# A graph layer's gather stage: the node inputs added by an identity product, the destinations unpacked first, the gathers written out

## The chip, the cores and the metric

One core of one Trainium2 chip runs the whole program. Its engines are PE (TensorE, matrix products), DVE (VectorE), ACT (ScalarE), POOL (GpSimd, which here issues all indirect DMAs) and SP (SyncE, which issues the plain DMAs). Each has an instruction queue of its own, and they wait for one another by semaphores. The metric is the time of one execution on the device in microseconds (us); less is better.

## What is computed

One layer over a graph of 6250 nodes with 256 features and 100,000 directed edges, in float32:

```
xn  = layernorm(x)
deg = count of edges with src != dst per dst node, plus 1
gnn[s] = sum over edges and self loops (s, d) of rsqrt(deg[s]) * rsqrt(deg[d]) * (xn @ W)[d]
mix = linear attention of xn (8 heads, elu + 1), times wo, plus bo
x1  = x + gnn + mix
out = x1 + mixture of 8 experts of layernorm(x1), the best two per node
```

## The kernel before

The nodes are 49 tiles of 128 (`NT`), `P` is 128 and `D` 256. In order of time the program sorts the edges into 25 groups by source (`NGR`; one group is two tiles of source nodes) while it normalizes x and makes keys, values and queries; then comes the **gather stage**, 461 to 1639 us, with which this change deals; then the second norm, the router and the experts.

Before the gather stage, `xn @ W` scaled by `rsqrt(deg)` is written to a DRAM tensor `table`, one row per node (SP, line 357). The sorted edges lie in DRAM as packed words of source and destination, in rows of four, 128 edges to a **chunk**, every chunk within one group. Rows that no edge has filled hold zeros; the places left over are padding edges with source and destination 6400, beyond the last table row, 6271.

Unpacking (lines 763 to 779, DVE; lines 1308 to 1314, PE). Line 365 brings the words to the chip, one chunk per row of 128. DVE splits them into sources and destinations, marks edges from a node to itself, clamps the destination to the last row (line 768) and forms `lo_f`, the source's place in its group. PE transposes `dst_f` and `lo_f` by 16 products with the identity, so that a chunk is a column of 128 partitions, and DVE copies the results to `dst_T` and `lo_neg`.

Then 880 chunks follow (`CHUNKS`), in batches of four (`UNROLL`), four batches to a step (`BATCHES`), 55 steps (`STEPS`). For each chunk:
- ACT copies four indices per batch from `dst_T` to a small buffer `idx_s` (`indices`, line 1131), once the gathers that used that buffer have landed.
- POOL issues one indirect DMA per chunk that gathers 128 rows of `table` into one of sixteen places in `G` (`gather_batch`, line 491). It waits for the indices, and, every second chunk, for PE to be done with the place (`seg`). This is a hardware loop over steps.
- ACT makes a matrix `OH` of ones and zeros that says which source a row belongs to (`onehots`, lines 1133 to 1139).
- PE multiplies (`sum_chunks`, line 1350): two f32 products per chunk, each 128x128 by 128x256 and in two passes, into one of four PSUM banks B[0] to B[3].
- DVE adds the bank, 128x512, to the accumulator `ACC` at the chunk's group (`add_sums`, line 794; the adds run through the helper at line 542). The group's number is unpacked on DVE's queue from a word that it loads for every batch (line 783).

The attention of one tile is woven into each of the first 49 steps: ACT `query_terms`, PE `query_products` (line 1324), DVE `divide` (after the step's first batch), PE `transpose_mix` (line 1331), ACT `transposed_mix`, PE `mix_out` (lines 1337 and 1339: bias, then two products with `wo`, into bank B[7]). In the next step DVE's `add_attention` (line 752) adds B[7] times `sdeg`, the root of the degree, to the tile's accumulator, after the second batch; after the third, `add_inputs` (line 760) adds x times `sdeg`. The order of DVE's step is written out by hand:

```
add_sums(i * BATCHES);      divide(i)
add_sums(i * BATCHES + 1);  add_attention(i - 1)
add_sums(i * BATCHES + 2);  add_inputs(i)
add_sums(i * BATCHES + 3)
```

In the loops, waits on a value that depends on the step go through the helper `when` (lines 102 to 111). In the later expert stage POOL's queue is written out without a loop: per tile a scatter (line 517), a gather of gates (line 510) and one of inputs (line 506).

Of the kernel before, what the change touches and what calls it, by code (L numbers as in the profile page):

```python
# [14 lines left out]
F32, BF16, I32, I16 = mybir.dt.float32, mybir.dt.bfloat16, mybir.dt.int32, mybir.dt.int16  # L15
# [4 lines left out]
P = 128  # L20
N_NODES = 6250
D = 256
# [79 lines left out]
def when(eng, tick, sem, value):  # L102

    if not isinstance(value, int):
        eng.wait_ge(sem, value)
        eng.sem_inc(tick, 1)
    elif value > 0:  # L110
        eng.wait_ge(sem, value)
# [13 lines left out]
def gps_layer(nc, x, src, dst, src_rest, dst_rest, gnn_w, wq, bq, wkv, bkv, wo, bo,  # L125
              wr, br, ln_gT, ln_bT, w1, b1, w2, b2, out):
    ctx = ExitStack()
    with ctx:
# [3 lines left out]
        def sem(name):  # L132
            return ctx.enter_context(nc.semaphore(name))

        def dram(name, shape, dt):
            return nc.dram_tensor(name, shape, dt, kind="Internal").ap()


        table = dram("table", [NT * P, D], F32)
        edge_rows = dram("edge_rows", [CPAD * RPC, ROW], I32)  # L140
# [16 lines left out]
        def piece(area, at, n, dt=F32):  # L157

            words = n if dt in (F32, I32) else (n + 1) // 2
            ap = area[:, at:at + words]  # L160
            return ap if dt == F32 else ap.bitcast(dt)
# [7 lines left out]
        def small(k, n=NT, dt=F32):  # L169
# [61 lines left out]

        raw, src_u, dst_u, same = (piece(BIG, 1024 * k, CPAD, I32) for k in range(4))
        raw3 = grid(BIG, 0, CG, P, I32)
        lo_f, dst_f, same_f = piece(BIG, 1024, CPAD), piece(BIG, 2048, CPAD), piece(BIG, 3072, CPAD)
        G = [grid(BIG, UNROLL * D * s, UNROLL, D) for s in range(BATCHES)]
# [3 lines left out]
        iota2 = piece(W2A, S2 + 3232, GN)  # L239
        idx_s = [piece(W2A, S2 + 3784 + UNROLL * s, UNROLL, I32) for s in range(BATCHES)]  # L240

# [63 lines left out]
            sem("q_terms"), sem("q_ps"), sem("q_mixed"), sem("q_mixedT_ps"), sem("q_mixedT"), sem("q_out"), sem("q_added"))  # L305
        raw_in, unpacked, unp_T, unp_out = sem("raw_in"), sem("unpacked"), sem("unp_T"), sem("unp_out")
        idx_ready, gath, onehot_ready, seg, added = (
            sem("idx_ready"), [[sem(f"gath{s}_{k}") for k in range(UNROLL // 2)] for s in range(BATCHES)], sem("onehot_ready"), sem("seg"), sem("added"))
        w1_in, w2_in, lnb_in, b2_in = [sem(f"w1_in{s}") for s in range(4)], sem("w2_in"), sem("lnb_in"), sem("b2_in")
# [18 lines left out]
        def _(sp):  # L328
# [4 lines left out]
            with nc.allow_non_contiguous_dma(reason="one edge per partition"):  # L333
# [15 lines left out]
                         ).then_inc(cleared_edges, 16)  # L349
            sp.dma_start(gates.rearrange("(c p) o -> c (p o)", p=P)[PICKS:PICKS + 1, :], zeros[0:1, 0:P]).then_inc(gates_out, 16)  # L350
            sp.wait_ge(cgroup_row, 1)
            sp.dma_start(chunk_groups.rearrange("(j p) -> j p", p=P // UNROLL), chunk_wI).then_inc(cgroup_out, 16)

            for k in range(TPARTS):
                sp.wait_ge(table_ready, k + 1)
                ts_ = slice(k * TPART, (k + 1) * TPART)
                sp.dma_start(table.rearrange("(t p) d -> p t d", p=P)[:, ts_, :], acc[:, ts_, :]).then_inc(table_out, 16)

# [64 lines left out]
        def _(pool):  # L423
# [59 lines left out]

            pool.wait_ge(table_out, 16 * TPARTS)

            def gather_batch(n, h):
                when(pool, tk_g, idx_ready, n + 1)
                for u in range(UNROLL):
                    if u % 2 == 0:
                        when(pool, tk_g, seg, (n - BATCHES) * UNROLL + u + 2)  # L490
                    pool.indirect_dma_start(G[h][:, u, :], None, table,  # L491
                                            bass.IndirectOffsetOnAxis(ap=idx_s[h][:, u:u + 1], axis=0)).then_inc(gath[h][u // 2], 16)

            for h in range(BATCHES):
                gather_batch(h, h)
            with pool.Fori(1, STEPS) as i:
                for h in range(BATCHES):
                    gather_batch(i * BATCHES + h, h)

# [38 lines left out]
        def _(dve):  # L538
            ch = Chain(dve, dve_steps)

            def tt(o, a, b, op):
                return dve.tensor_tensor(o, a, b, op)  # L542

            def ts(o, a, s1, op0, s2=None, op1=ALU.bypass):
                return dve.tensor_scalar(o, a, s1, s2, op0, op1)  # L545
# [208 lines left out]

            def add_inputs(t):

                dve.drain()
                a = acc[:, bass.ds(t, 1), :].rearrange("p o d -> p (o d)")
                xt = xr[:, bass.ds(t, 1), :].rearrange("p o d -> p (o d)")
                dve.scalar_tensor_tensor(out=a, in0=xt, scalar=sdeg[:, bass.ds(t, 1)], in1=a, op0=ALU.mult, op1=ALU.add)  # L760


            dve.wait_ge(raw_in, 16)
            ch.add(ts(src_u, raw, CODE, ALU.logical_shift_right))
            ch.add(ts(dst_u, raw, (1 << CODE) - 1, ALU.bitwise_and))
            ch.sync()
            ch.link(tt(same_f, src_u, dst_u, ALU.is_equal))
            ch.add(ts(dst_f, dst_u, float(NT * P - 1), ALU.min))
            ch.link(ts(raw, src_u, GN - 1, ALU.bitwise_and))

            ch.link(dve.scalar_tensor_tensor(out=lo_f, in0=same_f, scalar=float(2 * GN), in1=raw, op0=ALU.mult, op1=ALU.add))
            dve.sem_inc(unpacked, 1)
            for k in range(4):
                dve.wait_ge(unp_T, k + 1)
                n = min(512, CHUNKS - 512 * (k % 2))
                to = (dst_T, lo_neg)[k // 2][:, 512 * (k % 2):512 * (k % 2) + n]
                ch.add(dve.tensor_copy(to, B[k][:, 0:n]) if k < 2 else ts(to, B[k][:, 0:n], -1.0, ALU.mult))
            ch.sync()
            dve.sem_inc(unp_out, 1)
# [16 lines left out]
            def add_step(i):  # L796

                add_sums(i * BATCHES)
                if not isinstance(i, int) or i < NT:
                    divide(i)  # L800
                add_sums(i * BATCHES + 1)
                if not isinstance(i, int) or i > 0:
                    add_attention(i - 1)
                add_sums(i * BATCHES + 2)
                if not isinstance(i, int) or i < NT:
                    add_inputs(i)
                add_sums(i * BATCHES + 3)
# [4 lines left out]

            dve.wait_ge(table_out, 16 * TPARTS)
            add_step(0)
# [221 lines left out]
        def _(act):  # L1036
# [89 lines left out]

            def indices(n, h):

                for half in gath[h]:
                    when(act, tk_a, half, (n - h) * (32 // BATCHES))  # L1130
                act.copy(idx_s[h], dst_T[:, bass.ds(n * UNROLL, UNROLL)]).then_inc(idx_ready, 1)

            def onehots(n, h):
# [7 lines left out]
            def index_step(i):  # L1141
                for h in range(BATCHES):
                    if h == 3 and (not isinstance(i, int) or i > 0):
                        transposed_mix(i - 1)
                    indices(i * BATCHES + h + 1, (h + 1) % BATCHES)
                    if h < 3 and (not isinstance(i, int) or i < NT):
                        query_terms(i, h)
                    onehots(i * BATCHES + h, h)

            act.wait_ge(unp_out, 1)  # L1150
            indices(0, 0)
            index_step(0)
            with act.Fori(1, NT) as i:
                index_step(i)
            index_step(NT)
            with act.Fori(NT + 1, STEPS - 1) as i:
                for h in range(BATCHES):
                    indices(i * BATCHES + h + 1, (h + 1) % BATCHES)
                    onehots(i * BATCHES + h, h)
            for h in range(BATCHES):  # L1160
                if h < BATCHES - 1:
                    indices((STEPS - 1) * BATCHES + h + 1, h + 1)
                onehots((STEPS - 1) * BATCHES + h, h)


# [63 lines left out]
        def _(pe):  # L1229
# [77 lines left out]

            pe.wait_ge(unpacked, 1)
            for k in range(4):
                f = (dst_f, lo_f)[k // 2]  # L1310
                for j in range(4):
                    c = (k % 2) * 4 + j
                    last = nc.tensor.transpose(B[k][:, j * P:(j + 1) * P], f[:, c * P:(c + 1) * P], ident)
                last.then_inc(unp_T, 1)
# [19 lines left out]
            def mix_out(t):  # L1334
                when(pe, tk_t, q_mixedT, t + 1)
                when(pe, tk_t, q_added, t)
                mm(B[7][:, 0:D], ones_b, bias3[:, 2 * D:3 * D], start=True, stop=False)
                for g in range(KD):
                    last = mm(B[7][:, 0:D], mixedT[:, g, :], wo_s[:, g, :], start=False, stop=g == KD - 1)  # L1339
                last.then_inc(q_out, 1)  # L1340
# [161 lines left out]
```

## Time and profile before

| what | us |
|---|---|
| runs, median of 3 (lowest, highest) | 2579.94 (2579.68, 2581.04) |
| the profiled execution | 2579.8 |
| its span, first to last instruction | 2577.9 |
| PE busy in the span | 2203.5 |
| POOL busy | 1495.1 |
| DVE busy | 1313.0 |
| ACT busy | 1193.6 |

All times in rows count from the span's start. PE's busy time is that of pipelined products and their ends are modelled. A timeline row gives start, duration, engine, line, operation, the tiles written and read, a count, and in brackets the engine's idle time before it with what ended that; the name in the brackets is inferred, and it may be an engine that had been done long before.

### The profile page before, as it was taken

The page shows a single profiled execution, that of the slowest core. Times are in us where ns is not written, and L with a number is a line of the kernel's source. Part 1 is how long each engine was busy: PE and PEld are TensorE (multiplying, and loading weights), DVE is VectorE, ACT ScalarE, POOL GpSimd, SP SyncE. Part 2 cuts the span into 40 slices and gives each one's busy share as a digit, 9 for nine tenths or more (in the row PEclk, how much of TensorE's full clock was granted, in tenths as well). Part 3 has the DMA queues.
Part 4 walks back from the last instruction along what each step waited for, and adds up shares of the span by engine and source line. Part 5 has one row for each costly group of instructions (what it writes and reads, how often), then busy time and mean ns, then how long its engine had stood idle before and what let it go on. Part 6 is the DMA issues. An engine that isn't in the chain of part 4 may idle for free.

```text
span 2577.9 us, 54413 instructions
## 1 busy us (share of the span) xinstructions
PE 2203.5 (85%) x12043; PEld 1767.6 (69%) x12044; DVE 1313.0 (51%) x2361; ACT 1193.6 (46%) x3065; POOL 1495.1 (58%) x1493
## 2 busy tenths in 40 slices
PE   0999995788888888888888886658999999999995
PEld 0677774666666666666666664554999999999995
DVE  8799997555555555555555564543122222222221
ACT  2444442566666666666666664462233333322221
POOL 6766565677777777777777776101544444444442
PEclk9999997899999999999999999756999999999998
DMA  4000003233333333333333338455666666666664
GB/s 137 1 1 1 1 1 113 86 104 105 99 99 98 99 98 99 98 98 100 98 99 98 99 118 82 81 182 182 213 183 183 181 180 178 178 180 182 183 183 134
DMA packets 140076, 298.89 MB, mean 116 GB/s; under 512 B 31634, under 2 KB 80868, under 8 KB 139783
## 3 DMA queue, kind: packets, MB, share of 16 engines
q0 software_dynamic: 72672, 143.45, 22.5%
q1 hardware_dynamic: 67367, 155.03, 18.5%
q8 instruction: 12, 0.20, 0.0%
q14 instruction: 25, 0.20, 0.0%
HBM read 264.21 MB, written 40.58 MB: 118 GB/s over the span
## 4 chain that ended last, share of the span: by engine, by line
PE 58%; DVE 14%; DVEq 11%; issue 8%; DMA 4%; POOL 4%; ACT 0%; POOLq 0%; SPq 0%; ACTq 0%
PE B L1350 21%; PE B L1443 15%; PE B L1452 14%; DVE ACC L542 5%; DVEq L660 5%; DVE BIG L655 4%; DMA BIG<-table,W2A 3%; DVEq L783 2%; PE B L1339 2%; PE B L1324 2%; PE B L1412 1%; PE B L1390 1%; DVEq L791 1%; DVE W1A L542 1%; POOL W2A L467 1%
## 5 line engine op out<-in xcount | busy, mean ns | idle before, releaser
L491 POOL DMA_INDIRECT BIG<-table,W2A x880 | 834.3, 948 | 349.8 <-issue 223.5
L542 DVE TENSOR_TENSOR ACC<-ACC,B 128x512 f32 x880 | 605.4, 688 | 448.1 <-PE B L1350 320.7
L1350 PE MATMUL B<-BIG 128*128 128x256 f32 x1760 | 438.7, 393 | 106.8 <-DVE ACC L542 64.8
L1350 PE MATMUL B<-BIG,W2A 128*128 128x256 f32 x1760 | 437.6, 390 | 86.7 <-DVE ACC L542 55.7
L1040 ACT ACTIVATE BIG<-B,SMALL 128x128 f32<-128x128 f32 (+1 forms) x889 | 251.2, 388 | 524.0 <-PE B L1443 524.0
L1350 PEld LDWEIGHTS B<-BIG 128*128 128x128 f32 x1760 | 305.9, 190 | 238.9 <-issue 206.8
L1350 PEld LDWEIGHTS B<-BIG,W2A 128*128 128x128 f32 x1760 | 301.6, 189 | 199.7 <-issue 167.1
L1443 PEld LDWEIGHTS B<-BIG,W1A 128*128 128x128 f32 x3360 | 393.5, 193 | 7.9 <-DVE BIG L545 2.6
L1443 PE MATMUL B<-BIG,W1A 128*128 128x128 f32 x3360 | 394.3, 276 | 2.0 <-DVE BIG L545 2.0
L1452 PE MATMUL B<-W2A,BIG 128*128 x1680 | 380.2, 379 | 0.9 <-DVE BIG L542 0.7
L517 POOL DMA_INDIRECT sums<-BIG,SMALL x105 | 170.6, 1625 | 334.5 <-DMA sums<-BIG,SMALL 289.1
L1452 PEld LDWEIGHTS B<-W2A,BIG 128*128 128x128 f32 x1680 | 311.0, 190 | 39.4 <-issue 1.5
L1040 ACT ACTIVATE BIG<-W2A 128x256 f32<-128x256 f32 x440 | 187.6, 497 | 233.2 <-PE B L1350 233.2
L477 POOL DMA_INDIRECT edge_rows<-BIG x216 | 219.8, 1018 | 126.7 <-DVE BIG L665 64.6
L1040 ACT ACTIVATE W2A<-W2A 128x256 f32<-128x256 f32 x440 | 187.4, 496 | 203.8 <-PE B L1350 203.8
L545 DVE TENSOR_SCALAR BIG<-B,SMALL 128x128 f32<-128x128 f32 x210 | 76.5, 406 | 291.0 <-PE B L1431 291.0
L542 DVE TENSOR_TENSOR BIG<-B,W1A 128x256 f32<-128x256 f32 x105 | 44.6, 424 | 272.8 <-PE B L1452 272.8
L1040 ACT ACTIVATE BIG<-B 128x256 f32<-128x256 f32 (+1 forms) x172 | 65.7, 412 | 201.7 <-PE B L1256 166.3
L506 POOL DMA_INDIRECT BIG<-token_x,SMALL x53 | 51.1, 964 | 173.9 <-DVEq L982 158.0
L1040 ACT ACTIVATE BIG<-BIG,CONST 128x1024 f32<-128x1024 f32 x110 | 126.5, 1150 | 8.1
L1040 ACT ACTIVATE W2A<-W2A,CONST 128x1024 f32<-128x1024 f32 x110 | 126.4, 1149 | 8.1
L510 POOL DMA_INDIRECT BIG<-gates,SMALL x105 | 102.9, 980 | 32.0 <-issue 32.0
(214 smaller groups left out, 2198.0 us busy)
## 6 DMA issues: line engine op xcount, KB each, us to landing
W1A<-in_w SPq DMA_DIRECT2D x105, 1024.0 KB, 5.1
BIG<-table,W2A POOLq DMA_INDIRECT x880
W2A<-in_w SPq DMA_DIRECT2D x1, 8192.0 KB, 30.1
sums<-ACC SPq DMA_DIRECT2D x1, 6400.0 KB, 22.7
table<-ACC SPq DMA_DIRECT2D x7, 896.0 KB, 7.1
out_dram<-sums SPq DMA_DIRECT2D x1, 6250.0 KB, 21.9
W2A<-in_x SPq DMA_DIRECT2D x1, 6144.0 KB
token_x<-BIG SPq DMA_DIRECT2D x24, 256.0 KB, 2.1
```

The source lines that it names most:

```text
L477: pool.indirect_dma_start(edge_rows, bass.IndirectOffsetOnAxis(ap=row_at[s][:, j:j + 1], axis=0), stage_raw[s][:, ROW * j:ROW * (j + 1)], ...
L491: pool.indirect_dma_start(G[h][:, u, :], None, table, bass.IndirectOffsetOnAxis(ap=idx_s[h][:, u:u + 1], axis=0)).then_inc(gath[h][u // 2] ...
L510: pool.indirect_dma_start(slot_gate[:, t:t + 1], None, gates, bass.IndirectOffsetOnAxis(ap=slot_pick[:, t:t + 1], axis=0)).then_inc(gate_i ...
L517: pool.indirect_dma_start(sums, bass.IndirectOffsetOnAxis(ap=slot_row[:, t:t + 1], axis=0), y_out[t % 2], None, compute_op=ALU.add).then_i ...
L542: return dve.tensor_tensor(o, a, b, op)
L545: return dve.tensor_scalar(o, a, s1, s2, op0, op1)
L655: dve.max(eight, work)
L660: dve.drain()
L1040: return nc.scalar.activation(o, i, fn, **kw)
L1350: last = mm(B[u][:, k * D:(k + 1) * D], OH[h % 2][:, u, k * P:(k + 1) * P], G[h][:, u, :], start=True, stop=True)
L1443: last = mm(B[2 * s + c // 4][:, c % 4 * P:(c % 4 + 1) * P], w1_buf[s4][:, k, c * P:(c + 1) * P], x_inT[s][:, k, :], start=k == 0, stop=k ...
L1452: last = mm(B[7][:, 0:D], hidT[s][:, k, :], W2A[:, bass.ds(e * (KH * D) + k * D, D)], start=k == 0, stop=k == KH - 1)
```

## The change

Three things are changed, all in the gather stage.

1. `add_inputs` is removed from DVE's step. In `mix_out` PE multiplies the identity by the tile's x (`xr`) into the same bank B[7], between the bias and the products with `wo`, so that `add_attention` adds both.
2. DVE unpacks the destinations first: mask, copy to f32, and a semaphore for PE, which transposes them while DVE takes out the sources and compares. The two copies to `dst_T` come next and a new semaphore `dst_known`; only then are the sources masked and `lo_f` formed, transposed and copied. The clamp is gone: `table` has two more tiles of rows, which SP fills with zeros early on, and the padding edges read row 6400 there. Some temporary buffers have moved.
3. POOL's gathers are written out, 880 of them, with the index read from `dst_T` itself. `indices` and its buffers on ACT are removed, and with them the wait for the earlier gathers of the same buffer.

```diff
-        table = dram("table", [NT * P, D], F32)
+        table = dram("table", [(NT + 2) * P, D], F32)
...
+            sp.dma_start(table[NT * P:(NT + 2) * P, :].rearrange("(a p) d -> p a d", p=P), zeros.unsqueeze(1).to_broadcast([P, 2, D])
+                         ).then_inc(table_out, 16)
             sp.wait_ge(cgroup_row, 1)
...
-            pool.wait_ge(table_out, 16 * TPARTS)
-
-            def gather_batch(n, h):
-                when(pool, tk_g, idx_ready, n + 1)
-                for u in range(UNROLL):
-                    if u % 2 == 0:
-                        when(pool, tk_g, seg, (n - BATCHES) * UNROLL + u + 2)
-                    pool.indirect_dma_start(G[h][:, u, :], None, table,
-                                            bass.IndirectOffsetOnAxis(ap=idx_s[h][:, u:u + 1], axis=0)).then_inc(gath[h][u // 2], 16)
-
-            for h in range(BATCHES):
-                gather_batch(h, h)
-            with pool.Fori(1, STEPS) as i:
-                for h in range(BATCHES):
-                    gather_batch(i * BATCHES + h, h)
+            pool.wait_ge(table_out, 16 * (TPARTS + 1))
+
+            pool.wait_ge(dst_known, 1)
+            for c in range(CHUNKS):
+                h, u = c // UNROLL % BATCHES, c % UNROLL
+                if u % 2 == 0 and c >= BATCHES * UNROLL:
+                    pool.wait_ge(seg, c - BATCHES * UNROLL + 2)
+                pool.indirect_dma_start(G[h][:, u, :], None, table,
+                                        bass.IndirectOffsetOnAxis(ap=dst_T[:, c:c + 1], axis=0)).then_inc(gath[h][u // 2], 16)
...
-            ch.add(ts(src_u, raw, CODE, ALU.logical_shift_right))
-            ch.add(ts(dst_u, raw, (1 << CODE) - 1, ALU.bitwise_and))
-            ch.sync()
-            ch.link(tt(same_f, src_u, dst_u, ALU.is_equal))
-            ch.add(ts(dst_f, dst_u, float(NT * P - 1), ALU.min))
-            ch.link(ts(raw, src_u, GN - 1, ALU.bitwise_and))
-
-            ch.link(dve.scalar_tensor_tensor(out=lo_f, in0=same_f, scalar=float(2 * GN), in1=raw, op0=ALU.mult, op1=ALU.add))
+            ch.link(ts(dst_u, raw, (1 << CODE) - 1, ALU.bitwise_and))
+            ch.link(dve.tensor_copy(dst_f, dst_u))
             dve.sem_inc(unpacked, 1)
+            ch.link(ts(src_u, raw, CODE, ALU.logical_shift_right))
+            ch.link(tt(lo_f, src_u, dst_u, ALU.is_equal))
...
+            unpacked_half(0)
+            unpacked_half(1)
+            ch.sync()
+            dve.sem_inc(dst_known, 1)
+            ch.link(ts(src_u, src_u, GN - 1, ALU.bitwise_and))
+            ch.link(dve.scalar_tensor_tensor(out=lo_f, in0=lo_f, scalar=float(2 * GN), in1=src_u, op0=ALU.mult, op1=ALU.add))
+            dve.sem_inc(unpacked, 1)
+            unpacked_half(2)
+            unpacked_half(3)
...
-                if not isinstance(i, int) or i < NT:
-                    add_inputs(i)
...
-            pe.wait_ge(unpacked, 1)
             for k in range(4):
+                pe.wait_ge(unpacked, k // 2 + 1)
...
                 mm(B[7][:, 0:D], ones_b, bias3[:, 2 * D:3 * D], start=True, stop=False)
+                mm(B[7][:, 0:D], ident, xr[:, bass.ds(t, 1), :].rearrange("p o d -> p (o d)"), start=False, stop=False)
                 for g in range(KD):
```

`unpacked_half(k)` is the body of the old loop over the four copies. DVE's wait for `table_out` is raised by the same one write, and `index_step` on ACT loses its calls of `indices`.

## Rows read from the trace of the kernel before

**Rows 1.** Stretches (us from the start): each engine's busy time, clock, DMA share, GB/s.
```profile
core 0: us, PE busy (x) PEld busy (x) DVE busy (x) ACT busy (x) POOL busy (x), PEclk, DMA share, GB/s
461.00:657.00 196.00, 164.88 (x716) 121.30 (x717) 113.29 (x188) 125.23 (x267) 148.01 (x156) 0.97 0.35 104
657.00:1518.00 861.00, 736.81 (x3198) 523.34 (x3197) 513.65 (x850) 527.79 (x1131) 612.70 (x647) 1.00 0.33 98
1554.00:1639.00 85.00, 50.85 (x208) 37.45 (x208) 36.45 (x53) 36.35 (x71) 46.44 (x49) 1.00 0.87 78
```

**Rows 2.** Timeline of DVE over one step: start, duration, idle time before it.
```profile
1020.51 0.69 DVE L542 TENSOR_TENSOR ACC<-ACC,B 128x512 f32 x1 [0.90 <-PE B L1350]
...
1030.42 0.48 DVE L752 SCALAR_TENSOR_TENSOR ACC<-B,SMALL,ACC 128x256 f32 x1 [0.42 <-issue]
1031.67 0.69 DVE L542 TENSOR_TENSOR ACC<-ACC,B 128x512 f32 x1 [0.77 <-PE B L1350]
...
1034.83 0.69 DVE L542 TENSOR_TENSOR ACC<-ACC,B 128x512 f32 x1 [0.36 <-PE B L1350]
1035.83 0.48 DVE L760 SCALAR_TENSOR_TENSOR ACC<-W2A,SMALL,ACC  x1 [0.31 <-issue]
1037.08 0.69 DVE L542 TENSOR_TENSOR ACC<-ACC,B 128x512 f32 x1 [0.77 <-PE B L1350]
...
1041.82 0.69 DVE L542 TENSOR_TENSOR ACC<-ACC,B 128x512 f32 x1 [0.90 <-PE B L1350]
```

**Rows 3.** Timeline of PE in that step, and an unhindered batch near the attention's end.
```profile
1016.89 3.97 PE L1350 MATMUL B<-BIG 128*128 128x256 f32 x16 [1.44 <-DVE ACC L542]
...
1025.85 1.13 PE L1339 MATMUL B<-W1A 128*128 128x256 f32 x4
...
1519.63 3.62 PE L1350 MATMUL B<-BIG,W2A 128*128 128x256 f32 x16
```

**Rows 4.** Timeline of POOL: a gather early in the stage, then three in one step.
```profile
655.93 0.95 POOL L491 DMA_INDIRECT BIG<-table,W2A  x1 [0.30 <-issue]
...
684.47 0.94 POOL L491 DMA_INDIRECT BIG<-table,W2A  x1 [1.00 <-PE B L1350]
...
695.91 0.95 POOL L491 DMA_INDIRECT BIG<-table,W2A  x1 [0.30 <-PE B L1350]
...
700.07 0.95 POOL L491 DMA_INDIRECT BIG<-table,W2A  x1 [0.70 <-issue]
```

**Rows 5.** Timeline of all engines at the stage's start.
```profile
450.95 1.29 DVE L545 TENSOR_SCALAR BIG<-BIG 128x1024 int32<-128x1024 int32 x2 [11.59 <-DMA BIG<-edge_rows]
...
456.20 3.68 PE L1313 MATMUL B<-CONST,BIG 128*128 128x128 f32 x16 [35.87 <-DVEq L772]
457.36 0.69 DVE L777 CAST W2A<-B 128x512 int32<-128x512 f32 x1 [1.26 <-PE B L1313]
...
460.61 0.29 ACT L1131 COPY W2A<-W2A 128x4 int32<-128x4 int32 x2 [37.61 <-DVEq L779]
...
461.60 0.99 POOL L491 DMA_INDIRECT BIG<-table,W2A  x1 [23.18 <-ACT W2A L1131]
...
465.73 4.84 PE L1350 MATMUL B<-BIG 128*128 128x256 f32 x10 [5.85 <-DMA BIG<-table,W2A]
```

**Rows 6.** Timeline at the stage's end: a gather on POOL, DVE's last add.
```profile
1551.51 0.95 POOL L491 DMA_INDIRECT BIG<-table,W2A  x1 [0.30 <-issue]
...
1638.29 0.69 DVE L542 TENSOR_TENSOR ACC<-ACC,B 128x512 f32 x1 [0.36 <-issue]
```

**Rows 7.** Timeline before the stage: POOL's scatters, and DVE's multiplication of the table.
```profile
351.87 0.96 POOL L477 DMA_INDIRECT edge_rows<-BIG  x1 [0.30 <-issue]
...
424.02 13.56 DVE L542 TENSOR_TENSOR ACC<-ACC,SMALL 128x1792 f32<-128x1792 f32 x7
...
434.86 1.63 POOL L477 DMA_INDIRECT edge_rows<-BIG  x1 [0.30 <-issue]
```

**Rows 8.** Waits of POOL in the expert stage: us in total, times, longest.
```profile
POOL BIG L510 <- issue: 32.0, 105, 0.3
...
POOL sums L517 <- issue: 12.4, 3, 4.4
```

**Rows 9.** The chain that ended last, share of the span by line.
```profile
PE B L1350 21%; PE B L1443 15%; PE B L1452 14%; DVE ACC L542 5%; DVEq L660 5%; DVE BIG L655 4%; DMA BIG<-table,W2A 3%; DVEq L783 2%; PE B L1339 2%; PE B L1324 2%; PE B L1412 1%; PE B L1390 1%; DVEq L791 1%; DVE W1A L542 1%; POOL W2A L467 1%
```

More of the change, by code:

```diff
@@ L229, in gps_layer @@
         q_den = piece(W1A, S1 + 2480, KD * NH)
-        raw, src_u, dst_u, same = (piece(BIG, 1024 * k, CPAD, I32) for k in range(4))
+        raw, dst_f, dst_u = piece(BIG, 0, CPAD, I32), piece(BIG, 1024, CPAD), piece(BIG, 2048, CPAD, I32)
         raw3 = grid(BIG, 0, CG, P, I32)
-        lo_f, dst_f, same_f = piece(BIG, 1024, CPAD), piece(BIG, 2048, CPAD), piece(BIG, 3072, CPAD)
+        src_u, lo_f = piece(BIG, 4098, CPAD, I32), piece(W2A, S2 + 2 * CHUNKS, CPAD)
         G = [grid(BIG, UNROLL * D * s, UNROLL, D) for s in range(BATCHES)]
@@ L239, in gps_layer @@
         iota2 = piece(W2A, S2 + 3232, GN)
-        idx_s = [piece(W2A, S2 + 3784 + UNROLL * s, UNROLL, I32) for s in range(BATCHES)]
         NE = NT * E
@@ L305, in gps_layer @@
             sem("q_terms"), sem("q_ps"), sem("q_mixed"), sem("q_mixedT_ps"), sem("q_mixedT"), sem("q_out"), sem("q_added"))
-        raw_in, unpacked, unp_T, unp_out = sem("raw_in"), sem("unpacked"), sem("unp_T"), sem("unp_out")
-        idx_ready, gath, onehot_ready, seg, added = (
-            sem("idx_ready"), [[sem(f"gath{s}_{k}") for k in range(UNROLL // 2)] for s in range(BATCHES)], sem("onehot_ready"), sem("seg"), sem("added"))
+        raw_in, unpacked, unp_T, unp_out, dst_known = sem("raw_in"), sem("unpacked"), sem("unp_T"), sem("unp_out"), sem("dst_known")
+        gath, onehot_ready, seg, added = (
+            [[sem(f"gath{s}_{k}") for k in range(UNROLL // 2)] for s in range(BATCHES)], sem("onehot_ready"), sem("seg"), sem("added"))
         w1_in, w2_in, lnb_in, b2_in = [sem(f"w1_in{s}") for s in range(4)], sem("w2_in"), sem("lnb_in"), sem("b2_in")
@@ L356, in _ @@
                 ts_ = slice(k * TPART, (k + 1) * TPART)
-                sp.dma_start(table.rearrange("(t p) d -> p t d", p=P)[:, ts_, :], acc[:, ts_, :]).then_inc(table_out, 16)
+                sp.dma_start(table[0:NT * P, :].rearrange("(t p) d -> p t d", p=P)[:, ts_, :], acc[:, ts_, :]).then_inc(table_out, 16)
             sp.dma_start(wo_s, wo.rearrange("(k p) n -> p k n", p=P)).then_inc(wo_in, 16)
@@ L753, in add_attention, with unpacked_half @@
                                          op0=ALU.mult, op1=ALU.add).then_inc(q_added, 1)
[L755 to L760, printed above, removed]
-            dve.wait_ge(raw_in, 16)
-            ch.add(ts(src_u, raw, CODE, ALU.logical_shift_right))
-            ch.add(ts(dst_u, raw, (1 << CODE) - 1, ALU.bitwise_and))
-            ch.sync()
-            ch.link(tt(same_f, src_u, dst_u, ALU.is_equal))
-            ch.add(ts(dst_f, dst_u, float(NT * P - 1), ALU.min))
-            ch.link(ts(raw, src_u, GN - 1, ALU.bitwise_and))
-            ch.link(dve.scalar_tensor_tensor(out=lo_f, in0=same_f, scalar=float(2 * GN), in1=raw, op0=ALU.mult, op1=ALU.add))
+            dve.wait_ge(raw_in, 16)
+            ch.link(ts(dst_u, raw, (1 << CODE) - 1, ALU.bitwise_and))
+            ch.link(dve.tensor_copy(dst_f, dst_u))
             dve.sem_inc(unpacked, 1)
-            for k in range(4):
+            ch.link(ts(src_u, raw, CODE, ALU.logical_shift_right))
+            ch.link(tt(lo_f, src_u, dst_u, ALU.is_equal))
+            def unpacked_half(k):
                 dve.wait_ge(unp_T, k + 1)
@@ L811, in add_batches @@
                     add_sums(i * BATCHES + h)
-            dve.wait_ge(table_out, 16 * TPARTS)
+            dve.wait_ge(table_out, 16 * (TPARTS + 1))
             add_step(0)
@@ L1125, in transposed_mix @@
                 cp(mixedT, B[4][:, 0:D].rearrange("p (g n) -> p g n", g=KD)).then_inc(q_mixedT, 1)
[L1127 to L1131, printed above, removed]
             def onehots(n, h):
@@ L1144, in index_step @@
                         transposed_mix(i - 1)
-                    indices(i * BATCHES + h + 1, (h + 1) % BATCHES)
                     if h < 3 and (not isinstance(i, int) or i < NT):
@@ L1150, in _ @@
             act.wait_ge(unp_out, 1)
-            indices(0, 0)
             index_step(0)
@@ L1155, in _ @@
             index_step(NT)
-            with act.Fori(NT + 1, STEPS - 1) as i:
+            with act.Fori(NT + 1, STEPS) as i:
                 for h in range(BATCHES):
-                    indices(i * BATCHES + h + 1, (h + 1) % BATCHES)
                     onehots(i * BATCHES + h, h)
[L1160 to L1163, printed above, removed]
             def transposed_x2(j):
```

## The prediction

> **What bounds the kernel now.** I read the stretches first, then one step of the gather stage engine by engine, then its two ends. The stage from 461 to 1639 us is the only one that the change touches: 1178 us of the 2577.9, run as 880 chunks of 128 edges, sixteen to a step. Two things in the stretches [rows 1] matter. From 461 to 657 us POOL issues 156 gathers; from 657 to 1518 it is slower per gather (861 us for 647 of them, 1.33 us each), and the DMA engines are busy a third of the time. From 1554 the picture turns: DMA share 0.87 at only 78 GB/s, where 0.33 had carried 98.
>
> So what sets the 1.33? DVE. Its rows of one step [rows 2] run from 1020.51 to 1041.82, 21.31 us, and hold no real wait. The idle time is put down to PE, but look at PE [rows 3]: the batch that DVE adds from 1020.51 on ran there from 1016.89 to 1020.86, so its first quarter was ready near 1017.9, some 2.6 us before its add; and PE itself had stood 1.44 us for DVE. After the attention's add (30.42) the next batch's add starts 1.25 us later (31.67), after the inputs' add (35.83) again 1.25 (37.08): this is the time in which the queue loads the next group word, not the time of the operation before it.
>
> POOL is just behind. From 461.60 [rows 5] to 655.93 [rows 4] it starts 156 gathers, so 194.33 / 155 = **1.254 us** each, 20.06 us per sixteen, with nothing but its own 0.30 between them. From then on it waits in every step (1.00 us and, further on, 0.70 instead of the 0.30 [rows 4]): it has run sixteen chunks ahead and stands until PE frees a buffer. The waits of a step fill its 20.06 up to DVE's 21.31.
>
> The end: the gathers from 1554 to the last are 49 [rows 1], so the one at 1551.51 [rows 6] is number 880 - 49 - 2 = 829, counted from 0. About there the real edges run out; the padding chunks behind them name one table row for all 128 edges, and take 85 / 49 = 1.73 us each. DVE's last add is at 1638.29 [rows 6].
>
> **The change, part by part.** The sum is made on the profiled run, 2579.8 us (span 2577.9 and 1.9 around it), which is the runs' median of 2579.94 to 0.01%.
>
> *Inputs off DVE.* One operation per step goes, 49 in all. Today 34.83 (last add of a batch), 35.83 (inputs), 37.08 (next add): 2.25 us from add to add. Without the middle one the add at 34.83 is followed by the batch change. High end: the 1.25 of queue work covers the add's 0.69, as it covers the 0.48 today, and 1.00 us is saved. Low end: the 0.77 of idle stays whole behind the 0.69, and 2.25 - 1.46 = 0.79 is saved. I take 1.00, since the 1.25 is the same behind both operations of the rows. DVE's step becomes **20.31 us** (20.52 at the low end).
>
> *The identity product on PE.* Two f32 products 128x128x256 took 1.13 us together [rows 3], so one is 0.57, or 28 us over 49 steps. It lies in the time in which PE stands for DVE. A batch that nothing holds takes 3.62 [rows 3], four 14.5; the rest of a step is 21.31 - 4 x 3.97 - 1.44 = 4.0 at most; with the new product PE has 19.1 us of its own in 20.31. I cost it at nothing; if the cover were gone it would cost the 28.
>
> *Destinations first.* Raw words arrive at 450.95; six operations fill DVE until the transposes start at 456.20 (four of the short kind, 1.29 us for two, which leaves 2.67 for the compare and the fused one, 1.3 each); then come 16 transposes and four copies, ACT's copy of the indices at 460.61, and the first gather at 461.60 [rows 5]. After: one mask (0.65), one copy (0.65 to 1.2), eight transposes, whose first half was there 1.16 after their start; meanwhile DVE shifts (0.65) and compares (1.3), ending near 454.4; two copies (0.69 for the first, less for the shorter second) end near 455.7. The step from the index copy's start to the gather's was 1.0; without ACT between I take 0.9, so the first gather is at **456.6**, 5.0 us sooner (bounds 3.5 and 5.5). The other half of the unpacking (0.65, 1.3, eight transposes, two copies) ends near 460.6, as now, and ACT builds its first matrices then. PE starts when those are ready, not at 465.73, when the first data had landed.
>
> *Here a rule speaks against the change.* Gathers will now be issued while DVE still unpacks. When DVE multiplied the table, POOL's scatters took 1.63 us instead of 0.96 [rows 7]. At 0.67 each, three gathers inside the remaining 3.1 us or so of DVE work would lose 2.0 us; the 156 gathers beside DVE's adds lost nothing. I take zero and keep 2.0 as bound. The Trainium skill's page "SBUF — State Buffer" (section "SBUF: two separate sides") says that a DMA issued by GpSimd cannot get its descriptors written while a two-port DVE operation holds the shared port; by that all 3.1 us would be lost, and the sum would be 2528. The scatters of the rows were lengthened, not stopped, so the trace bears it out in part.
>
> *ACT's index copies* (220, with their waits) go; ACT is not what anyone waits for past the start, so nothing. *POOL's loop written out*: the gather stays the same instruction, and in the written-out stretch later POOL's gap before L510 is 32.0 / 105 = 0.305 us [rows 8], so 1.254 stays. Upper bound: three of the waits before L517 there are unexplained, 12.4 us together [rows 8]; one such 4.1 us per 105 instructions would be 880 / 105 x 4.1 = 34 us. *The two tiles of zero rows* are one more write of 256 KB on SP's queue, ahead of a wait that it stands at anyway and long before the stage; nothing. The added count in the waits of POOL and DVE for the table is met by then. Queued behind POOL's new wait for the destinations are only the gathers themselves.
>
> **Sum.** What is late next? With POOL's 20.06 under DVE's 20.31, POOL gains 0.25 us per step on DVE, 12 us over 49 steps, on top of the 9 us at most (456.6 to 465.73) by which it starts ahead of PE. Together that meets the limit of sixteen chunks (20 us) only as the attention ends, and the later steps have no attention. So POOL hardly waits: gather 829 starts at 456.6 + 829 x 1.254 = 1496.2 instead of 1551.51, 55.3 us sooner. The padding tail follows unchanged (same row for all, only another row), and so does everything behind 1639. Taking off 0.5 us for late waits: 2579.8 - 54.8 = **2525.0**. If DVE saves only 0.79, POOL stands for about 10 us: 2535. If the first gather gains nothing: 2530.
>
> **Rivals.**
> - *POOL stalls in straight-line code.* For it: 880 instructions instead of sixteen, and the unexplained 4.1 us. Against: 105 regular gaps without one stall. 2525 + 34 = 2559; with a third of that 2536.
> - *PE takes what DVE gives.* The mixing product is longer, attention's add comes later, and DVE waits. For it: PE is busy 86% of 657 to 1518 [rows 1]. Against: DVE ran 2.6 us behind PE within the step [rows 2, 3]. 2525 + 28 = 2553.
> - *Slower: PE was the pace all along.* The chain of waits gives PE's L1350 21% of the span, against DVE's 5% [rows 9]. Then nothing is saved on DVE, 28 us are added, 5 won at the start: 2603. It decides if PE's own step is over 20.3 us; the rows give 19.1 with the product.
> - *The tail is cured.* If the row of zeros is not read as slowly as the clamped row is, 49 chunks at 1.254 save 49 x 0.48 = 23 us: 2502. Against: still one row for all.
> - *It doesn't do what it says:* the gather starts no sooner, because the transposes wait for something else; that is the 2530 above, inside the forecast.
>
> **How the numbers follow.** Forecast (2516 to 2537) 0.70; POOL stalls 0.11; PE shares 0.10; slower 0.05; tail cured 0.03; about no change, from several of these at once, 0.01. The range from 2512 to 2556 takes the forecast, most of the PE case and half of the POOL case, and leaves out some 0.15. A measurement of this kernel can tell about 0.2% (5 us) from no change; beyond that faster 0.93, same 0.02, slower 0.05.
>
> **What would show it.** In the new profile: no L760 row on DVE; 20.3 us between DVE's steps; the identity product's f32 passes (0.57 for the two) ahead of the mixing ones; the first gather near 456.6; 1.25 us from gather to gather almost to the end, with few waits for PE; the DMA share rising near 1499; the last add near 1584. Wrong would be: gaps of several us on POOL with no releaser; DVE waiting at the attention's add; a step of 21 us or more; a tail of another length than 85 us.

## The result and the profile after

The changed kernel takes **2523.02 us**, median of four runs (2522.35 to 2525.25); the kernel before, beside it, 2580.35 (four runs). The ratio is 0.9779 (95% interval 0.9762 to 0.9796). The forecast was 2525.0 in 2512 to 2556. The profiled execution took 2523.16, its span 2521.3. In the changed code the gather is line 493, DVE's helpers are 538 and 541, the attention's add 748, PE's chunk products 1330, the identity product 1317, the transposes 1292.

The stage's start, timeline of all engines (start, duration, idle time before it); the rows answer to [rows 5]:

```profile
450.40 0.69 DVE L541 TENSOR_SCALAR BIG<-BIG 128x1024 int32<-128x1024 int32 x1 [11.30 <-DMA BIG<-edge_rows]
451.13 0.69 DVE L753 CAST BIG<-BIG 128x1024 f32<-128x1024 int32 x1
451.94 1.97 PE L1292 MATMUL B<-CONST,BIG 128*128 128x128 f32 x8 [31.86 <-DVEq L754]
...
453.96 1.14 DVE L762 CAST W2A<-B 128x512 int32<-128x512 f32 x2
...
455.96 0.98 POOL L493 DMA_INDIRECT BIG<-table,W2A  x1 [19.74 <-DVEq L767]
455.99 1.24 DVE L769 SCALAR_TENSOR_TENSOR W2A<-W2A,BIG 128x1024 f32<-128x1024 f32 x1
457.25 0.95 POOL L493 DMA_INDIRECT BIG<-table,W2A  x1 [0.31 <-issue]
...
463.52 4.75 PE L1330 MATMUL B<-BIG 128*128 128x256 f32 x13 [4.22 <-ACT BIG L1033]
...
465.71 0.69 DVE L538 TENSOR_TENSOR ACC<-ACC,B 128x512 f32 x1 [5.83 <-PE B L1330]
```

The first gather starts 5.56 us after the raw words arrive, against 10.65 before, and PE then waits for ACT's matrices, no longer for data.

One step on DVE, and the stage's last add (timeline of DVE):

```profile
1001.06 0.48 DVE L748 SCALAR_TENSOR_TENSOR ACC<-B,SMALL,ACC 128x256 f32 x1 [0.42 <-issue]
1002.31 0.69 DVE L538 TENSOR_TENSOR ACC<-ACC,B 128x512 f32 x1 [0.77 <-PE B L1330]
...
1005.47 0.69 DVE L538 TENSOR_TENSOR ACC<-ACC,B 128x512 f32 x1 [0.36 <-PE B L1330]
1006.72 0.69 DVE L538 TENSOR_TENSOR ACC<-ACC,B 128x512 f32 x1 [0.56 <-PE B L1330]
...
1021.38 0.48 DVE L748 SCALAR_TENSOR_TENSOR ACC<-B,SMALL,ACC 128x256 f32 x1 [0.42 <-issue]
...
1580.04 0.69 DVE L538 TENSOR_TENSOR ACC<-ACC,B 128x512 f32 x1 [0.36 <-issue]
```

Where 2.25 us lay between the adds around the inputs [rows 2], 1.25 lie now (1005.47 to 1006.72). The step is 1021.38 - 1001.06 = **20.32 us** (21.31 before).

The same step on PE:

```profile
996.50 0.70 PE L1317 MATMUL B<-W2A,CONST 128*128 x2
997.03 1.03 PE L1319 MATMUL B<-W1A 128*128 128x256 f32 x4
997.89 3.99 PE L1330 MATMUL B<-BIG 128*128 128x256 f32 x16
...
1003.29 4.11 PE L1330 MATMUL B<-BIG,W2A 128*128 128x256 f32 x16 [1.19 <-DVE ACC L538]
1007.80 4.01 PE L1330 MATMUL B<-BIG 128*128 128x256 f32 x16 [0.40 <-DVE ACC L538]
```

The identity product's two passes are there; the mixing product starts 0.53 us after them, and PE still stands 1.19 and 0.40 us for DVE.

POOL: a gather at the time of the first one in [rows 4], the same gather as in [rows 6], and between them the first wait of any size:

```profile
655.97 0.95 POOL L493 DMA_INDIRECT BIG<-table,W2A  x1 [0.30 <-issue]
...
1371.46 0.94 POOL L493 DMA_INDIRECT BIG<-table,W2A  x1 [0.62 <-PE B L1330]
...
1494.05 0.95 POOL L493 DMA_INDIRECT BIG<-table,W2A  x1 [0.31 <-issue]
```

The last is gather 829, **57.5 us** sooner than the 1551.51 of [rows 6]. That is the gain: 86.0 us then pass to the last add (1580.04), where 86.8 did, and 941.2 to the end, where 939.6 did. Summed over all gathers, what POOL idles beyond its own 0.30 fell from 61.2 us to 5.4.

The stretches, as in [rows 1]:

```profile
657.00:1400.00 743.00, 671.77 (x2962) 488.23 (x2963) 445.82 (x731) 465.43 (x880) 561.45 (x594) 1.00 0.35 105
1500.00:1584.00 84.00, 50.02 (x206) 36.67 (x204) 40.01 (x66) 34.58 (x59) 43.47 (x46) 0.99 0.88 75
```

POOL's 594 gathers in 743 us are 1.25 us each: in the body of the stage nothing holds it, and its own gather sets the pace. PEclk is 1.00 there, as before. The padding stretch is as slow as it was (0.87 at 78).

### The profile page after: what moved, and what is told of

It reads as the page before. It is cut to its first block, busy times and chain, and to the rows that moved or that the text cites. A ratio compares the mean times of both kernels' runs of the same rounds, so it can differ in the third digit from the quotient of the medians.

```text
span 2521.3 us, 52177 instructions
## 1 busy us (share of the span) xinstructions
PE 2209.7 (88%) x12141; PEld 1789.7 (71%) x12142; DVE 1289.2 (51%) x2312; ACT 1173.2 (47%) x2845; POOL 1489.7 (59%) x1493
## 3 DMA queue, kind: packets, MB, share of 16 engines
q1 hardware_dynamic: 67639, 155.29, 19.1%
## 4 chain that ended last, share of the span: by engine, by line
PE 62%; DVE 12%; DVEq 9%; issue 7%; POOL 5%; DMA 3%; ACT 0%; SPq 0%; POOLq 0%; ACTq 0%
PE B L1330 20%; PE B L1423 15%; PE B L1432 14%; DVE ACC L538 5%; DVEq L656 3%; POOL BIG L493 3%; DVE BIG L651 3%; DMA BIG<-table,W2A 2%; DVEq L786 2%; PE B L1303 2%; PE B L1392 1%; DVEq L778 1%; PE B L1370 1%; PE B L1235 1%; PE B L1268 1%
## 5 line engine op out<-in xcount | busy, mean ns | idle before, releaser
L1330 PE MATMUL B<-BIG 128*128 128x256 f32 x1760 | 430.6, 389 | 48.2 <-DVE ACC L538 18.5
```

The lines of the kernel that those rows point to most:

```text
L1330: last = mm(B[u][:, k * D:(k + 1) * D], OH[h % 2][:, u, k * P:(k + 1) * P], G[h][:, u, :], start=True, stop=True)
```

## The experiments

The times are medians, with the lowest and highest run. The ratio is to the kernel before in the same session: 2580.4 for the first four experiments, 2580.37 for the others, 2578.03 for the ten products.

### The product alone

The kernel before with only its first part changed: `add_inputs` gone, the product added; loop, index copies and old order of unpacking stay.

```diff
-                if not isinstance(i, int) or i < NT:
-                    add_inputs(i)
...
+                mm(B[7][:, 0:D], ident, xr[:, bass.ds(t, 1), :].rearrange("p o d -> p (o d)"), start=False, stop=False)
```

> The kernel before with one part of the change: x is added by the identity product, DVE's inputs add is gone; unpacking, clamp, POOL's loop and ACT's index copies stay. Theory (DVE sets the step, POOL is next): the step falls from 21.31 to 20.3 us, the first gather stays at 461.6, POOL no longer waits and reaches gather 829 near 1501; the time is 2530 us (2526 to 2536), that is 50 of the 57 us that the whole change brought. Rival A (POOL's loop has stalls of its own: every 133 us it stood 1.95 us with no releaser): eight of them come onto the path, 2543 us. Rival B (DVE is relieved, but without the earlier start POOL cannot keep ahead and PE waits for data): over 2555 us.

Measured: 2528.49 us (2527.55 to 2529.68), ratio 0.98 (0.9787 to 0.9814); first gather at 462.23, step 20.20 us, gather 829 at 1499.84. One part of three brings 51.9 of the 57.3 us.

### The other two parts, without the product

The changed kernel with the inputs added by DVE again, and no product.

> The changed kernel with that one part undone: x is added by DVE again, no identity product; destinations first, 880 gathers written out. Theory: the step is 21.3 us again, POOL is soon sixteen chunks ahead and stands; the earlier start gives only the 2.2 us by which the first add comes sooner: 2577 us (2573 to 2580). Rival (the gathers' form and start are worth something by themselves in the body): under 2568 us.

Measured: 2571.22 us (2568.88 to 2574.11), ratio 0.9967 (0.9955 to 0.9979); step 21.32. DVE's operation does set the step. But the time is below the expected 2573 to 2580, and above the rival's 2568: 9.2 us under the kernel before is more than an earlier start brings, so something else in these two parts counts. It is followed up below.

### Loop and index copies back

The changed kernel with POOL's loop and ACT's `indices` as before; the destinations are still unpacked first.

> The changed kernel with POOL's hardware loop and ACT's index copies back; the destinations are still unpacked first and x is still added by the product. Theory: POOL's gather costs 1.25 us in either form, and the first batch of gathers starts as early (near 457); the second batch waits for ACT, which by then waits for the sources (near 460.5). 2525 us (2522 to 2530). Rival (the loop's stalls of 1.95 us every 133 us return and lie on the path): 2536 us or more.

Measured: 2529.48 us (2527.15 to 2529.75), ratio 0.9801 (0.9787 to 0.9814), 6.5 above the changed kernel, though its first gather is at 456.75. The time is inside the expected range, but not for the expected reason: gather 829 is at 1500.32, as late as with the product alone. It comes 6.3 us later than in the changed kernel, though the first gather is only 0.8 later; the rest is lost on POOL. One part is single stalls of 1.18, 1.21 and 1.83 us (at 1101, 1228 and 1355). Another is the first gather itself, which took 1.82 us (timeline of all engines):

```profile
456.48 1.22 DVE L776 SCALAR_TENSOR_TENSOR W2A<-W2A,BIG 128x1024 f32<-128x1024 f32 x1
456.75 1.82 POOL L494 DMA_INDIRECT BIG<-table,W2A  x1 [18.34 <-ACT W2A L1131]
```

It started 0.26 us behind a DVE operation that reads two tensors of the on-chip memory (SBUF), and ended 0.86 us after it. The scatters of [rows 7] show the same: the one at 434.86 starts inside one of the seven multiplications of the table,

```profile
433.63 2.02 DVE L542 TENSOR_TENSOR ACC<-ACC,SMALL 128x1792 f32<-128x1792 f32 x1
```

and ends at 436.49, 0.84 us after it.

The last part, 1.6 us, is that the other gathers take 947.5 ns in the mean instead of 945.6. That is no property of the loop: with the product alone, in the same loop, it is 945.7, and the written-out kernels lie between 945.3 and 947.0.

### The product's price

The changed kernel without the line of the identity product; the nodes' own x is then missing from the sum.

> The changed kernel without the identity product: the nodes' own x is left out of the sum, nothing else differs. Theory (the product lies in time in which PE stands for DVE): 2523 us, within 3. Rival (the product is paid for): 49 x 0.53 = 26 us less, 2497 us; something between if part of it is paid.

Measured: 2522.34 us (2521.09 to 2525.17), ratio 0.978 (0.9765 to 0.9795), 0.7 under the changed kernel and inside its spread; step 20.32. The product costs nothing that can be measured.

### How much cover PE has

Six, then ten, products of a zero matrix with x behind the identity product, into the same bank.

```diff
                 mm(B[7][:, 0:D], ident, xr[:, bass.ds(t, 1), :].rearrange("p o d -> p (o d)"), start=False, stop=False)
+                for _ in range(6):
+                    mm(B[7][:, 0:D], zeros[:, 0:P], xr[:, bass.ds(t, 1), :].rearrange("p o d -> p (o d)"), start=False, stop=False)
```

> The changed kernel with six more products of a zero matrix with x behind the identity product (they add zeros): 6 x 0.53 = 3.2 us more on PE in each of 49 steps. Theory (PE's own work in a step of 20.33 is some 17 us: it stands 1.6 us, and its batches take 4.0 instead of 3.62 because DVE holds them): the step grows little, 2523 to 2540 us. Rival (only the visible 1.6 us is cover): 1.6 us more per step, 2601 us. Rival (no cover at all): 49 x 3.2, 2679 us.

> Ten zero products a step behind the identity product, where six left the step at 20.33 us. With six, the rows of PE's step show 0.17 us of standing, and two batches of 3.90 and 4.13 where an unheld one takes 3.62, 0.79 together. The four products more cost 4 x 0.46 = 1.84. Theory 1 (the whole cover is what stands plus what the held batches are stretched by, 0.96): PE becomes the bound and the step is 20.33 + 1.84 - 0.96 = 21.2 us, 48 x 0.88 = 42 us over the kernel after, near 2566. Theory 2 (the stretch is no cover, only the standing is): 20.33 + 1.84 - 0.17 = 22.0 us, near 2603. Theory 3 (PE is still far from the bound): 20.33 us and at most 3 us more than with six, near 2529.

Measured with six: 2526.68 us (2524.02 to 2527.12), ratio 0.9793 (0.9778 to 0.9808), 3.7 above the changed kernel; step 20.33. With ten: **2608.14** (2607.22 to 2608.6), ratio 1.0113 (1.0097 to 1.013); step 22.01. Timeline of PE: with six, the group of 12 passes that holds the zero products; then with ten, a step from one bias product to the next, with the zero products inside the group of 20:

```profile
1019.11 2.75 PE L1319 MATMUL B<-W2A 128*128 x12
```

```profile
1018.84 0.28 PE L1316 MATMUL B<-W1A 3*128 3x256 bf16 x1
1019.04 0.70 PE L1317 MATMUL B<-W2A,CONST 128*128 x2
1019.58 4.48 PE L1319 MATMUL B<-W2A 128*128 x20
...
1032.19 3.87 PE L1332 MATMUL B<-BIG 128*128 128x256 f32 x16
1035.89 1.11 PE L1303 MATMUL B<-W1A 128*128 128x132 f32 x8
1036.84 4.09 PE L1332 MATMUL B<-BIG,W2A 128*128 128x256 f32 x16
1040.86 0.28 PE L1316 MATMUL B<-W1A 3*128 3x256 bf16 x1
```

and DVE beside it:

```profile
1025.30 0.48 DVE L748 SCALAR_TENSOR_TENSOR ACC<-B,SMALL,ACC 128x256 f32 x1 [2.11 <-PE B L1321]
...
1037.82 0.69 DVE L538 TENSOR_TENSOR ACC<-ACC,B 128x512 f32 x1 [0.36 <-issue]
...
1047.32 0.48 DVE L748 SCALAR_TENSOR_TENSOR ACC<-B,SMALL,ACC 128x256 f32 x1 [2.11 <-PE B L1321]
```

The groups of 12 and of 20 passes take 2.75 and 4.48, so one product costs 1.73 / 4 = 0.43. Six of them fit into the step of 20.33; the next four lengthen it by 1.68, nearly all of their 1.73. So the cover was 2.6 us, of which the visible waits show 1.6. Theory 2 held.

With ten, DVE stands 2.11 us at the attention's add, for the mixing product. But PE is not the whole pace. No PE row is preceded by a wait, yet a row merges many passes, and a short wait inside it does not show. Taken singly, the passes of a batch start 0.22 us apart; in the batch at 1036.84 the first pass for the third bank starts 0.49 behind the one ahead of it:

```profile
1038.84 0.45 PE L1332 MATMUL B<-BIG,W2A 128*128 128x256 f32 x1
```

DVE's add of that bank in the batch before is the one at 1037.82, which ends at 1038.51, 0.33 us earlier. So the path of the step runs through DVE's adds, the end of this batch, the added products and the attention's add. As PE is held in the step, 22.01 - 10 x 0.43 = **17.7 us** is an upper bound for PE's own step in the changed kernel, which takes 20.33 a step.

### Padding spread over a tile of rows

The changed kernel with padding edge e of a chunk reading row 6400 + e, instead of all reading row 6400. Both are rows of zeros.

```diff
-            ch.link(dve.tensor_copy(dst_f, dst_u))
+            spread = lo_f.rearrange("p (c e) -> p c e", e=P)
+            ch.link(dve.scalar_tensor_tensor(out=spread, in0=dst_u.rearrange("p (c e) -> p c e", e=P), scalar=float(PAD),
+                                             in1=iota.unsqueeze(1).to_broadcast([P, CG, P]), op0=ALU.is_ge, op1=ALU.mult))
+            ch.link(tt(dst_f, dst_u, lo_f, ALU.add))
```

> The changed kernel, but a padding edge in column e of its chunk names row 6400 + e of the zero rows instead of row 6400: two DVE operations of 1.24 us in place of the copy of 0.69. Theory (the padding tail is slow because 128 reads go to one row): the last chunks go at POOL's 1.25 us, 49 x 0.48 = 23 us less, 2 us more at the start: 2503 us (2499 to 2508). Rival A (the tail is slow for another reason, such as reads from rows written once and late, or the DMA queue being full): 2525 us. Rival B (only part of the conflict goes, since the rows lie in one stretch of memory): 2510 to 2520 us.

Measured: **2508.68 us** (2507.49 to 2510.66), ratio 0.9725 (0.9712 to 0.9738): the best version, 14.3 us under the changed kernel, though just above the expected 2499 to 2508. The stretch from 1510 to 1550 us of the changed kernel:

```profile
1510.00:1550.00 40.00, 23.64 (x97) 17.25 (x96) 16.66 (x25) 17.11 (x30) 30.24 (x32) 1.00 0.99 79
```

and of this one:

```profile
1510.00:1550.00 40.00, 32.36 (x133) 23.35 (x132) 23.89 (x35) 23.37 (x42) 30.25 (x33) 1.00 0.35 105
```

As many gathers are issued, but the DMA engines, busy throughout at 79 GB/s, now carry 105 with a third of their time, as in the body. From gather 829 to the last add 69.9 us pass instead of 86.0. Against that 16.1, the two longer operations delay the first gather by 1.8 us (457.76) and gather 829 by 1.3. The end is not quite cured, as PE's last waits in this run show:

```profile
1553.04 1.97 PE L1333 MATMUL B<-BIG 128*128 128x256 f32 x8 [0.44 <-DMA BIG<-table,W2A]
1556.50 1.97 PE L1333 MATMUL B<-BIG 128*128 128x256 f32 x8 [1.50 <-DMA BIG<-table,W2A]
1559.69 1.97 PE L1333 MATMUL B<-BIG,W2A 128*128 128x256 f32 x8 [1.22 <-DMA BIG<-table,W2A]
1562.80 1.97 PE L1333 MATMUL B<-BIG,W2A 128*128 128x256 f32 x8 [1.15 <-DMA BIG<-table,W2A]
```

By the kernel's text the last chunks are words of zero, which the edit does not spread: they all read row 0.

### What the two other parts bring

The 9.2 us of the second experiment called for a closer look at POOL in the kernel before. ACT's index copies, and the gathers behind them (timelines of ACT, of POOL, and at the attention's end of PE and DVE, kernel before):

```profile
1034.40 0.18 ACT L1131 COPY W2A<-W2A 128x4 int32 x1
...
1039.81 0.18 ACT L1131 COPY W2A<-W2A 128x4 int32 x1
...
1492.95 0.18 ACT L1131 COPY W2A<-W2A 128x4 int32 x1
```

```profile
1035.53 0.95 POOL L491 DMA_INDIRECT BIG<-table,W2A  x1 [0.47 <-issue]
...
1040.94 0.95 POOL L491 DMA_INDIRECT BIG<-table,W2A  x1 [0.70 <-issue]
...
1494.12 0.95 POOL L491 DMA_INDIRECT BIG<-table,W2A  x1 [0.99 <-PE B L1350]
```

```profile
1485.63 4.01 PE L1350 MATMUL B<-BIG 128*128 128x256 f32 x16 [1.39 <-DVE ACC L542]
```

```profile
1510.57 0.69 DVE L542 TENSOR_TENSOR ACC<-ACC,B 128x512 f32 x1 [0.86 <-PE B L1350]
```

The gathers with a longer idle time start 0.95 to 0.98 us after the end of a copy. They do not wait for a place, although the bracket of the last one names PE: its place was free when PE had done the first half of the batch at 1485.63, near 1487.6, and it starts 6.5 us after that. It is the same in all 102 waits over 0.33 us between gather 16 and gather 829, the six stalls named in the last section left out: the copy had ended less than 1 us before, and the place had been free for 6.1 to 6.5 us. The copies lie in ACT's queue among the matrices, and so hold POOL's lead below the sixteen places. At the attention's end (chunk 784) the gather leads its add by 1510.57 - 1494.12 = 16.4 us in the kernel before. Two kernels follow from that: the second experiment's with POOL waiting for the whole unpacking (only the written-out gathers left), and the changed kernel with the same wait (only the early start undone). In both the edit on POOL is

```diff
-            pool.wait_ge(dst_known, 1)
+            pool.wait_ge(unp_out, 1)
```

> x added by DVE as before, and POOL's first gather held back until the whole unpacking is done, as before; what is left of the change is the gathers written out with the index read directly, without ACT's copies. Theory (before, POOL stood for ACT's index copies, which stand behind ACT's matrices, so its lead was held at some 12 chunks; written out it leads by 16): the step stays 21.3, the lead at the end of the attention is 22 us instead of 16.5, and 6 us are won there: 2574 us (2571 to 2577). Rival (the lead is won by the early start alone): 2580 us, within 2.

> The changed kernel with one part undone: POOL's first gather waits for the whole unpacking (near 461 instead of 456), all else stays. Theory (with the product on PE POOL's row of gathers is the path from the first gather to the padding, and it has no slack to make up a late start): all 5 us are lost, 2528 us (2526 to 2531). Rival (DVE's 20.33 us step is still the path and POOL catches up): 2523 us, within 2.

Measured: the first 2572.96 us (2572.18 to 2575.27), ratio 0.9972 (0.9961 to 0.9983); the second 2527.59 (2526.43 to 2529.2), ratio 0.9796 (0.9782 to 0.9809). Chunk 784 with only the written-out gathers, on POOL and on DVE:

```profile
1488.71 0.94 POOL L493 DMA_INDIRECT BIG<-table,W2A  x1 [0.81 <-PE B L1339]
```

```profile
1511.10 0.69 DVE L538 TENSOR_TENSOR ACC<-ACC,B 128x512 f32 x1 [0.57 <-PE B L1339]
```

Its add is as late as before, since DVE sets the step at 21.33, but the lead is 22.4 us instead of 16.4. Behind the attention the adds are quicker and catch up with POOL, so the 6 us of lead become time; the written-out gathers alone give 7.4 us. The early start alone is worth 4.6 us where POOL is the path (against the changed kernel) and 1.7, hardly more than the spread of the runs, where DVE is (the second experiment against this one). The parts do not add: 51.9 and 7.4 and 1.7 make 61.0, and the whole change gives 57.3. Copies and loop were not taken out apart; that it was the copies that held POOL is read from the rows above.

## Why the prediction was right

- **DVE's queue sets the step.** Held. The larger of the two savings came: 20.33 us a step against 20.31 forecast, the next add 1.25 us behind the one before it. That the 1.25 is the loading of the group word was not tried by itself.
- **The identity product at nothing.** Held, but for a cover that was sized too small. One product is 0.43 us in a row of them, and 0.53 from its start to the next product's in the changed kernel, not 0.57; and PE's own step is at most 17.7, not 19.1: the working took all time between the batches for PE's own. The rival in which the mixing product is longer, the attention's add comes later and DVE waits is real as a mechanism: ten more products made it so, and the kernel slower than before.
- **The first gather at 456.6.** It came at 455.96, in an execution whose raw words arrived 0.55 us earlier; counted from those it was 5.56 us against 5.65. The late start costs 4.6 us, close to the 5.0 forecast.
- **The lock that speaks against it.** The zero came by luck: it hung on an order of starts that the working did not look at. The gather at 455.96 started 0.02 us ahead of DVE's two-input operation at 455.99 and took 0.98, as the first gather before did [rows 5]; the three behind it took 0.95, 0.95 and 0.94. With the loop and the copies back the operation was first by 0.26, and the gather took 1.82. The working also misread [rows 7] as 0.67 more for each scatter; they wait for the end of the operation that they start in. The page of the Trainium skill, "SBUF — State Buffer" (section "SBUF: two separate sides"), says that of a DVE operation with two SBUF inputs and a GpSimd operation that reads SBUF the one that starts first has the shared port for its whole instruction, and the other is blocked. The rows of the third experiment and [rows 7] agree with it. Neither the bound of 2.0 us nor the 3.1 of the rule fits: even there only one gather was held, by one operation, and it cost 0.84.
- **POOL written out without a stall.** Held: 1038.09 us from gather 0 to gather 829 make 1.252 each against 1.254, and no idle time over 0.33 us between two of them before 1371, when the sixteen places are first full. Written out is no guarantee: see the stalls in the last section.
- **POOL hardly waits.** Held: gather 829 at 1494.05 against 1496.2, 0.64 of it from the start, the rest from the pace, and a gather's mean time differs by as much between kernels of either form. The meeting with the limit of sixteen came earlier than thought (near 1371, about 0.3 us a step), and costs less than 2 us.
- **The tail.** Unchanged, as forecast: 86.0 us. That a row of zeros cures nothing but a tile of such rows does was shown by spreading the padding.

**The step that was wrong** is one of the first part: that POOL, from 657 us on, "stands until PE frees a buffer", and with it that the index copies on ACT cost nothing ("ACT is not what anyone waits for past the start"). POOL stood for those copies while its places were free, its lead was 16.4 us and not that of sixteen chunks, and taking the copies away with the loop is worth 7.4 us by itself. It did the total no harm, since the forecast let POOL run free from end to end in any case.

## What to carry to other kernels

After an engine is relieved, find who runs free next and follow that one's row from its first instruction to its last: here POOL's 829 steps of 1.25 us gave the time within 2 us. Before a wait is put down to one thing, look when each thing that is waited for was ready: here the places had been free for 6 us when POOL seemed to wait for them. Cover is best measured by adding work until the step grows, since the waits in a trace show only part of it (1.6 of 2.6 us). Indices that point many descriptors at one row can cost more than the change at hand; spread them over as many rows.

## What the runs showed of the hardware

- **Many reads of one row.** Chunks whose 128 reads name one row of the table keep the DMA engines 99% busy at 79 GB/s; the same reads over 128 rows keep them 35% busy at 105. Per byte that is 3.8 times the engine time.
- **A gather behind a DVE operation with two SBUF inputs.** It ends 0.84 to 0.86 us after the operation where it started in the midst of one (the third experiment and [rows 7]). With only the written-out gathers, three that start 0.25, 0.28 and 0.31 us into DVE's add of the inputs take 1.06, 1.02 and 1.00 us; those that start 0.36 us into it, or in its first 0.09, take 0.95.
- **Single stalls at every hundredth gather.** In the kernel before, POOL idles 1.48 to 1.95 us ahead of gathers 213, 313, 413, 513, 613 and 713, with no releaser that would explain it. With the loop back in the changed kernel it is gathers 513, 613 and 713 (1.18, 1.21 and 1.83 us), with the product alone 713 (1.33). The changed kernel, written out, shows none; but written out with the inputs added by DVE, gathers 313, 413, 513 and 713 have 0.50 instead of 0.30 us (the second experiment; the same with the late start). They are longer in the loop, but come without it too; what comes round every hundred gathers was not found.
- **A gap that comes and goes.** In the changed kernel one add of a step has an idle time of 0.48 us before it where the others have 0.36; with the product alone the same place has 0.36, and the step is 20.20 us instead of 20.33. DVE's order of work is the same in both. The kernel before has the 0.48 too.
